# Perceiver-like stack on one core: score tiles of the wide cross-attention issued in pairs, query products over six steps, two waits of TensorE filled

## The chip, the cores and the metric

The kernel runs on one core of a Trainium2 chip, in one launch. The metric is the device time of that launch in microseconds. An execution under the profiler gives the trace; its times are microseconds from the start of the span.

## The reference

Input: latents `x` (8 x 64 x 256) and a context (8 x 1024 x 192). Four blocks, each of a cross-attention, a self-attention and a feed-forward, each with a layer norm before it and a residual add after it:

```python
x = x + _L0_xattn_ref(_layernorm(x), ctx, ...)   # one head
x = x + _L0_attn_ref(_layernorm(x), ...)         # 16 heads of 16, shared keys
x = x + _L0_ffn_ref(_layernorm(x), ...)
x = x + _L1_xattn_ref(_layernorm(x), ctx, ...)   # wide: 16 heads of 64
...
x = x + _L2_xattn_ref(_layernorm(x), ctx, ...)   # wide: 16 heads of 64
```

The change is about the two wide cross-attentions and about `_L0_attn_ref`. A wide one is:

```python
q = (x @ Wq).reshape(b, n, h, d).transpose(0, 2, 1, 3)
k = (context @ Wk).reshape(b, -1, h, d).transpose(0, 2, 1, 3)
v = (context @ Wv).reshape(b, -1, h, d).transpose(0, 2, 1, 3)
attn = softmax(einsum('bhid,bhjd->bhij', q, k) * scale)
out = einsum('bhij,bhjd->bhid', attn, v).transpose(0, 2, 1, 3).reshape(b, n, h * d)
return out @ Wo + bo
```

## The kernel before, in words

The program is written engine by engine, each with its own order of work, written out by hand. Semaphores tie the engines together. `Sync` (SP) issues nearly all DMAs, in one queue.

**The wide layers** (`wide(k)`, k = 0 and 1, on TensorE, ScalarE and VectorE) project the queries through the key weights rather than the context. Eight pairs of heads give queries 0 to 7 (`queries`, L1854). For each head group hh (0 to 7) two products with the key weights (`keys(hh, 0)`, `keys(hh, 1)`, L1874) give the rows that are multiplied with the transposed context. ScalarE makes a high half of them in 16 bits (`keys_high`, L631), VectorE the low half (`keys_low`, L1114). `key_slot` says at which step they are made, `key_banks` in which banks of PSUM.

There are 64 score tiles of 128 rows x 1024 keys, 8 for each head group: tile t = 2g + j, where g is the attention group (32 of them). `scores(t)` (L1890 to L1896) writes banks 2(t%2) and 2(t%2)+1, one bank for each n: in each, four products over 128 rows (h0 and l0 are high and low part of rows 0 to 127 of the context's width, h1 and l1 those of the rest), called whole products here; then one product over 64 rows, with l1, in each bank. These two half products use different halves of the array and run at the same time. Tiles alternate between two pairs of banks, so tile t waits for the exp of tile t-2.

Each tile passes through VectorE and ScalarE: row max (`rowmax`, L1118), `exp` (L639), reciprocal of the sum (`recip`, L1124 and L1125), high part of the weights (`weights_high`, L648), low part (`weights_low`, L1131), then VectorE transposes in blocks (`block_transpose`, L1136). SP stores the tile to DRAM in four pieces (`store_blocks`, L470), and fetches both tiles of a group back, turned (`fetch_turned`, L483). `weights_high(t)` waits for the stores of tile t-3. `attend_high(g)` (L1910 to L1912) and `attend_low(g)` (L1923, in column tiles of 64, and L1929) multiply them with the context; ScalarE copies the result (`attended`, L657). After the four groups of a head group, `heads` (L1942) applies the value weights, VectorE copies that (L1141), and `out` (L1948) applies the output weights at the end.

TensorE's steps s = 0 to 64 in the order of before: `scores(s)`; for s < 3 two queries; `attend_high((s-7)/2)` at odd s from 7, `attend_low((s-8)/2)` at even s from 8; `keys` where `key_slot` is s; `heads(s/8-2)` at multiples of 8 from 16. Then `attend_high(29)`, `attend_low(29)`, `out` of two token tiles, and so on. The output weights (`L1x_o`, `L2x_o`) are loaded by SP after tile 61 has been stored and the fetch of group 30 issued (L458), since they take a slot of the ring that is in use till then. ScalarE and VectorE have steps of the same number: at step s ScalarE does exp and high part of tile s, then a query's scaling (s < 3), `attended`, `keys_high`; VectorE does row max of s, low part of s-1, reciprocal of s, block transpose of s-1, a query's scaling (L1108), `keys_low` at `key_slot`+1, and `heads`.

**Grouped self-attention of block 0** (`self16(0)`) goes through eight units u: `scores(u)` (L2227, L2234), softmax on VectorE and ScalarE, `turn(u)` (a transpose, L2245), `attend(u)`. `project` makes queries, `ready` waits till they are copied. `keep_clock(n, b)` (L1792) issues n matmuls of 512 columns on constants into bank b, whose result nobody reads.

Of the kernel before, what the change touches and what calls it, by code (L numbers as in the profile page):

```python
# [71 lines left out]
def build(nc, widths, units_d, experts_d, const_d, ctx_d, x_d, out_d):  # L72
    ctx = ExitStack()
    with ctx:
# [317 lines left out]
        def key_banks(hh, j):  # L392

            return bank(4 if hh == 0 and j == 1 else 6, 2, 8, 64)

        def key_slot(hh, j):

            return 3 + 2 * j if hh == 1 else 8 * hh - 4 + 2 * j

# [206 lines left out]
        def _(act):  # L606
# [15 lines left out]
            def wide(k):  # L622
# [40 lines left out]
                for s in range(72):  # L663
                    if s < 64:
                        exp(s)
                        weights_high(s)
                    if s < 3:
                        scale_queries(2 * s + 2)
                    if s >= 9 and s % 2 == 1:
                        attended((s - 9) // 2)  # L670
                    for hh in range(1, 8):
                        for j in range(2):
                            if s == key_slot(hh, j):
                                keys_high(hh, j)
# [359 lines left out]
        def _(dve):  # L1034
# [70 lines left out]
            def wide(k):  # L1105
# [41 lines left out]
                for s in range(65):  # L1147
# [6 lines left out]
                    if s >= 1:  # L1154
                        block_transpose(s - 1)
                    if s < 3:
                        scale_queries(2 * s + 3)
                    for hh in range(1, 8):
# [617 lines left out]
        def _(pe):  # L1776
# [63 lines left out]
            def wide(k):  # L1840
# [17 lines left out]
                def keys(hh, j):  # L1858
                    r, hf = 2 * (hh // 2) + j, hh % 2
                    o = key_banks(hh, j)  # L1860
                    if hh == 0:
                        pe.wait_ge(*((xa_qsd, 4 * k + 1) if j else (xa_qsa, 4 * k + 1)))
                        pe.wait_ge(xa_qsd, 4 * k + 1)
                    elif hh == 1:
                        pe.wait_ge(xa_qsa, 4 * k + 4)
                        pe.wait_ge(xa_qsd, 4 * k + 4)
# [11 lines left out]
                def scores(t):  # L1878
# [8 lines left out]
                    h1, l1 = key_columns(k, hh, j, 1, bb)  # L1887
                    for n in range(2):
                        o = ps[:, 2 * (t % 2) + n, :]
                        PE.matmul(o, h0, key_blocks(0, b, n), start=True, stop=False)  # L1890
                        PE.matmul(o, h0, key_blocks(2, b, n), start=False, stop=False)  # L1891
                        PE.matmul(o, l0, key_blocks(0, b, n), start=False, stop=False)  # L1892
                        PE.matmul(o, h1, key_blocks(1, b, n), start=False, stop=False)  # L1893
                    for n in range(2):
                        o = ps[:, 2 * (t % 2) + n, :]
                        ins = PE.matmul(o, l1[half(n)], key_blocks(1, b, n, half(n)), start=False, stop=True)  # L1896
                    ins.then_inc(xa_S, 1)

                def attend_high(g):
                    b = g % 8  # L1900
                    pe.wait_ge(xa_turned[g % 2], turned_value(k, g))
                    if g >= 2:

                        pe.wait_ge(xa_Zs, 32 * k + g - 1)
# [53 lines left out]
                for s in range(65):  # L1958
                    if s < 64:
                        scores(s)  # L1960
                    if s < 3:
                        queries(2 * s + 2)
                        queries(2 * s + 3)
                    if s >= 7 and s % 2 == 1:
# [3 lines left out]
                    for hh in range(1, 8):  # L1968
                        for j in range(2):
                            if s == key_slot(hh, j):  # L1970
                                keys(hh, j)
                                if hh == 7 and j == 1:
                                    pe.wait_ge(xa_A, 16 * k + 16)
                                    release(1)
                    if s >= 16 and s % 8 == 0:
                        if s == 16:
                            loaded(f"{L}_v")
                        heads(s // 8 - 2)
                attend_high(29)
                attend_low(29)  # L1980
                loaded(f"{L}_o")
# [184 lines left out]
            def self16(k):  # L2166
# [105 lines left out]
                if k == 0:  # L2272
# [28 lines left out]
                    shared_values(1, 1)  # L2301
                    project(1, 1, 2, wq, 0)
                    project(1, 1, 2, wq, 1)
                    turn(4)
                    ready(1, 2, 2)
                    scores(6)
# [634 lines left out]
```

## Time and profile before

| what | us |
|---|---|
| median of 3 runs | 1330.73 |
| lowest and highest run | 1323.06, 1332.35 |
| profiled execution, its device time | 1330.26 |
| its span | 1328.5 |
| TensorE matmuls busy | 1244.1 (94% of the span) |
| VectorE busy | 918.6 (69%) |
| ScalarE busy | 616.5 (46%) |
| granted clock of TensorE, mean | 0.982 |

Busy time of TensorE counts a matmul from its start to the end of its pipeline, so matmuls overlap in the rows; how long one takes is read from the start of one to the start of the next. The names are PE for TensorE, PEld for its weight loads, DVE for VectorE, ACT for ScalarE. A row of the timeline may merge several instructions of one line (x8); "[1.43 <-DVE ...]" is idle time ahead of the row and what ended it. An f32 matmul is recorded as two.

### The profile page before, as it was taken

To read this page: it belongs to the slowest core of one execution; us is meant where nothing else is said; L and a number is where in the kernel's file an instruction comes from. 1 tells how busy PE (TensorE), PEld (TensorE's weight loads), DVE (VectorE), ACT (ScalarE), POOL (GpSimd) and SP (SyncE) were. 2 spreads that over 40 slices of the span, in tenths; PEclk is the share of its full clock that TensorE was granted. 3 is DMA by queue.
4 is the path that set the end of the run, shared out by engine and by line. 5 is a ranking of instruction groups with operands and counts; after the bars stand their busy time and mean duration, and the time that the engine had idled before them with its cause. 6 is when DMAs were issued, how large, how long until landed. Compare 5 with 4: busy or idle time off the path is not lost.

```text
span 1328.5 us, 22697 instructions
## 1 busy us (share of the span) xinstructions
PE 1244.1 (94%) x9156; PEld 828.7 (62%) x9156; DVE 918.6 (69%) x1695; ACT 616.5 (46%) x916; POOL 66.9 (5%) x88
## 2 busy tenths in 40 slices
PE   7888899899999999989898899999999999999798
PEld 4556597355555555668584455555555668998375
DVE  7655612799889898345535898989988267882556
ACT  6612311566666666213113666666665024652233
POOL 0000001000000000010001000000000001240100
PEclk9997999999999999999999999999999999999999
DMA  7210164268777767720210577777777514655000
GB/s 259 95 64 1 64 236 176 82 206 252 230 215 222 222 220 225 257 116 1 100 64 32 179 233 232 215 219 223 238 210 242 214 80 177 271 205 203 0 2 17
DMA packets 106072, 215.87 MB, mean 162 GB/s; under 512 B 10864, under 2 KB 76528, under 8 KB 98544
## 3 DMA queue, kind: packets, MB, share of 16 engines
q1 hardware_dynamic: 104816, 206.03, 47.4%
q0 software_dynamic: 1152, 8.39, 1.7%
q8 instruction: 73, 1.20, 0.4%
q14 instruction: 31, 0.25, 0.1%
HBM read 146.74 MB, written 67.63 MB: 161 GB/s over the span
## 4 chain that ended last, share of the span: by engine, by line
PE 70%; DVE 20%; ACT 3%; DMA 2%; issue 2%; POOL 2%; SPq 1%; ACTq 0%; DVEq 0%; POOLq 0%
PE ps L238 20%; PE ps L1910 4%; PE ps L1890 4%; PE ps L1929 4%; PE ps L1911 4%; PE ps L1891 4%; PE ps L1892 4%; PE ps L1893 4%; PE ps L1912 4%; PE ps L1896 3%; PE ps L1854 2%; PE ps L1942 2%; PE ps L1923 2%; PE ps L1874 2%; PE ps L1948 2%
## 5 line engine op out<-in xcount | busy, mean ns | idle before, releaser
L648 ACT ACTIVATE wk<-wk 128x1024 f16<-128x1024 f32 x128 | 185.0, 1445 | 67.4 <-DVE wk L1125 47.0
L639 ACT ACTIVATE wk<-ps,wk 128x1024 f32<-128x1024 f32 x128 | 142.6, 1114 | 149.1 <-DVE wk L1118 149.1
L1118 DVE TENSOR_REDUCE wk<-ps 128x1 f32<-128x1024 f32 x128 | 155.0, 1211 | 54.0 <-PE ps L1896 54.0
L1131 DVE SCALAR_TENSOR_TENSOR wk<-wk 128x1024 f16<-128x1024 f32 x128 | 179.3, 1400 | 4.8 <-ACT wk L648 4.8
L1136 DVE STREAM_TRANSPOSE wk<-wk 128x1024 f32<-128x1024 f32 x128 | 156.9, 1226 | 0.1
L238 PE MATMUL ps<-wk,ring 128*128 128x128 f32 (+4 forms) x920 | 122.1, 290 | 6.7 <-ACT wk L776 2.1
L238 PEld LDWEIGHTS ps<-wk,ring 128*128 128x128 f32 (+1 forms) x920 | 109.3, 192 | 15.9 <-issue 4.8
L238 PE MATMUL ps<-ring,wk 128*128 128x256 f32 (+2 forms) x456 | 100.6, 375 | 3.6 <-DVE wk L1280 1.4
L1890 PE MATMUL ps<-ctx_T,ring 128*128 128x512 f16 x256 | 97.9, 383 | 3.6 <-DVE ring L1114 3.0
L1891 PE MATMUL ps<-ctx_T,ring 128*128 128x512 f16 x256 | 97.6, 381 | 0.0
L1892 PE MATMUL ps<-ctx_T,ring 128*128 128x512 f16 x256 | 97.4, 381 | 0.0
L1893 PE MATMUL ps<-ctx_T,ring 128*128 128x512 f16 x256 | 97.2, 380 | 0.0
L238 PEld LDWEIGHTS ps<-ring,wk 128*128 128x128 f32 (+2 forms) x456 | 79.4, 189 | 15.5 <-DVE wk L1280 1.9
L1792 PE MATMUL ps<-cst 128*128 128x512 f16 x318 | 79.5, 396 | 9.7 <-DMA cst<-consts 6.9
L1910 PE MATMUL ps<-ring,ctx_keys 128*128 128x256 f16 x320 | 87.6, 274 | 0.0
L1911 PE MATMUL ps<-ring,ctx_keys 128*128 128x256 f16 x320 | 87.2, 273 | 0.0
L1912 PE MATMUL ps<-ring,ctx_keys 128*128 128x256 f16 x320 | 86.2, 269 | 0.0
L541 POOL TENSOR_TENSOR rstd<-rstd,cst 128x3 f32<-128x3 f32 (+1 forms) x26 | 19.5, 753 | 1158.2 <-DVE rstd L1051 1151.8
L238 PE MATMUL ps<-xn_both,ring 128*128 128x256 f32 (+2 forms) x220 | 59.0, 425 | 3.9 <-DVE xn_both L1083 3.9
L657 ACT ACTIVATE wk<-ps 128x512 f32<-128x512 f32 x64 | 36.5, 570 | 54.6 <-PE ps L1929 48.7
L1792 PEld LDWEIGHTS ps<-cst 128*128 128x128 f16 x318 | 30.6, 101 | 47.5 <-issue 11.3
L238 PE MATMUL ps<-wk 128*32 128x64 f32 (+7 forms) x676 | 56.6, 250 | 3.8 <-ACT wk L799 2.0
(344 smaller groups left out, 2080.2 us busy)
## 6 DMA issues: line engine op xcount, KB each, us to landing
blocks<-wk SPq DMA_DIRECT2D x512, 128.0 KB, 3.9
ring<-blocks SPq DMA_DIRECT2D x40, 1024.0 KB, 5.7
ring<-units SPq DMA_DIRECT2D x34, 1024.0 KB, 6.1
xn_both<-blocks SPq DMA_DIRECT2D x22, 1024.0 KB, 5.7
ring<-experts SPq DMA_DIRECT2D x16, 1024.0 KB, 5.3
ring<-context SPq DMA_DIRECT2D x16, 384.0 KB, 4.0
wk<-context SPq DMA_DIRECT2D x16, 384.0 KB, 5.2
wk<-blocks SPq DMA_DIRECT2D x2, 1024.0 KB, 5.0
```

Of the source, the lines that this page charges most:

```text
L238: return PE.matmul(out, lhsT, rhs, start=start, stop=stop)
L639: ACTE.activation(blocks, bank(2 * (t % 2), 2, 4, 128), ACT.Exp, bias=WNM[:, t % 4:t % 4 + 1], accum_out=WRS[:, t % 4:t % 4 + 1]).then_inc ...
L648: ACTE.activation(weight_halves(t)[0], WXP[:, t % 2, :], ACT.Identity, scale=WRI[:, t % 4:t % 4 + 1]).then_inc(xa_PH, 1)
L1118: DVE.tensor_reduce(WNM[:, t % 4:t % 4 + 1], bank(2 * (t % 2), 1024), X, ALU.max, negate=True).then_inc(xa_max, 1)
L1131: DVE.scalar_tensor_tensor(low, WXP[:, t % 2, :], WRI[:, t % 4:t % 4 + 1], high, ALU.mult, ALU.subtract).then_inc(xa_PL, 1)
L1136: DVE.transpose(packed_weights(t), packed_weights(t)).then_inc(xa_block, 1)
L1890: PE.matmul(o, h0, key_blocks(0, b, n), start=True, stop=False)
L1891: PE.matmul(o, h0, key_blocks(2, b, n), start=False, stop=False)
L1892: PE.matmul(o, l0, key_blocks(0, b, n), start=False, stop=False)
L1893: PE.matmul(o, h1, key_blocks(1, b, n), start=False, stop=False)
L1910: PE.matmul(z1, CN[:, kt, hi:hi + 128], h, start=n == 0, stop=False)
L1911: PE.matmul(z1, CN[:, kt, lo:lo + 128], h, start=False, stop=False)
```

## The change

Six things are changed.

1. TensorE issues `scores(s)` and `scores(s+1)` back to back at even s. The even tile has its half products last, the odd tile first, so that the four half products of a pair are adjacent.
2. Queries 2 to 7 come one at each of steps 0 to 5, not two at each of steps 0 to 2; their scaling on ScalarE (even ones) and VectorE (odd ones) moves with them.
3. `keys(1, 0)` uses bank 4, so it no longer waits for the queries' scaling; `keys(1, 1)` moves from step 5 to step 6. `attend_high(0)`, which writes bank 4, waits for `keys_low(1, 0)`.
4. `heads(6)` comes after `attend_high(29)`.
5. In `self16(0)` there are six `keep_clock` matmuls ahead of the second half of a projection, and
6. four after `turn(4)`, with a wait for `sa_ys`, because they write the bank that `attend` uses.

```diff
--- before.py
+++ after.py
@@ -391,11 +391,11 @@
 
         def key_banks(hh, j):
 
-            return bank(4 if hh == 0 and j == 1 else 6, 2, 8, 64)
+            return bank(4 if (hh, j) in ((0, 1), (1, 0)) else 6, 2, 8, 64)
 
         def key_slot(hh, j):
 
-            return 3 + 2 * j if hh == 1 else 8 * hh - 4 + 2 * j
+            return 3 + 3 * j if hh == 1 else 8 * hh - 4 + 2 * j
 
         def hi_columns(g):
 
@@ -664,8 +664,8 @@
                     if s < 64:
                         exp(s)
                         weights_high(s)
-                    if s < 3:
-                        scale_queries(2 * s + 2)
+                    if s < 6 and s % 2 == 0:
+                        scale_queries(s + 2)
                     if s >= 9 and s % 2 == 1:
                         attended((s - 9) // 2)
                     for hh in range(1, 8):
@@ -1153,8 +1153,8 @@
                         recip(s)
                     if s >= 1:
                         block_transpose(s - 1)
-                    if s < 3:
-                        scale_queries(2 * s + 3)
+                    if s < 6 and s % 2 == 1:
+                        scale_queries(s + 2)
                     for hh in range(1, 8):
                         for j in range(2):
                             if s == key_slot(hh, j) + 1:
@@ -1861,7 +1861,7 @@
                     if hh == 0:
                         pe.wait_ge(*((xa_qsd, 4 * k + 1) if j else (xa_qsa, 4 * k + 1)))
                         pe.wait_ge(xa_qsd, 4 * k + 1)
-                    elif hh == 1:
+                    elif hh == 1 and j == 1:
                         pe.wait_ge(xa_qsa, 4 * k + 4)
                         pe.wait_ge(xa_qsd, 4 * k + 4)
                     if hh >= 2:
@@ -1885,20 +1885,34 @@
                         pe.wait_ge(xa_exp, 64 * k + t - 1)
                     h0, l0 = key_columns(k, hh, j, 0, bb)
                     h1, l1 = key_columns(k, hh, j, 1, bb)
-                    for n in range(2):
-                        o = ps[:, 2 * (t % 2) + n, :]
-                        PE.matmul(o, h0, key_blocks(0, b, n), start=True, stop=False)
-                        PE.matmul(o, h0, key_blocks(2, b, n), start=False, stop=False)
-                        PE.matmul(o, l0, key_blocks(0, b, n), start=False, stop=False)
-                        PE.matmul(o, h1, key_blocks(1, b, n), start=False, stop=False)
-                    for n in range(2):
-                        o = ps[:, 2 * (t % 2) + n, :]
-                        ins = PE.matmul(o, l1[half(n)], key_blocks(1, b, n, half(n)), start=False, stop=True)
-                    ins.then_inc(xa_S, 1)
+                    odd = t % 2 == 1
+
+                    def whole():
+                        for n in range(2):
+                            o = ps[:, 2 * (t % 2) + n, :]
+                            PE.matmul(o, h0, key_blocks(0, b, n), start=not odd, stop=False)
+                            PE.matmul(o, h0, key_blocks(2, b, n), start=False, stop=False)
+                            PE.matmul(o, l0, key_blocks(0, b, n), start=False, stop=False)
+                            ins = PE.matmul(o, h1, key_blocks(1, b, n), start=False, stop=odd)
+                        return ins
+
+                    def halves():
+                        for n in range(2):
+                            o = ps[:, 2 * (t % 2) + n, :]
+                            ins = PE.matmul(o, l1[half(n)], key_blocks(1, b, n, half(n)), start=odd, stop=not odd)
+                        return ins
+                    if odd:
+                        halves()
+                        whole().then_inc(xa_S, 1)
+                    else:
+                        whole()
+                        halves().then_inc(xa_S, 1)
 
                 def attend_high(g):
                     b = g % 8
                     pe.wait_ge(xa_turned[g % 2], turned_value(k, g))
+                    if g == 0:
+                        pe.wait_ge(xa_AL, 16 * k + 3)
                     if g >= 2:
 
                         pe.wait_ge(xa_Zs, 32 * k + g - 1)
@@ -1956,11 +1970,11 @@
                 keys(0, 0)
                 keys(0, 1)
                 for s in range(65):
-                    if s < 64:
+                    if s < 64 and s % 2 == 0:
                         scores(s)
-                    if s < 3:
-                        queries(2 * s + 2)
-                        queries(2 * s + 3)
+                        scores(s + 1)
+                    if s < 6:
+                        queries(s + 2)
                     if s >= 7 and s % 2 == 1:
                         attend_high((s - 7) // 2)
                     if s >= 8 and s % 2 == 0:
@@ -1972,11 +1986,12 @@
                                 if hh == 7 and j == 1:
                                     pe.wait_ge(xa_A, 16 * k + 16)
                                     release(1)
-                    if s >= 16 and s % 8 == 0:
+                    if s >= 16 and s % 8 == 0 and s < 64:
                         if s == 16:
                             loaded(f"{L}_v")
                         heads(s // 8 - 2)
                 attend_high(29)
+                heads(6)
                 attend_low(29)
                 loaded(f"{L}_o")
                 pe.wait_ge(xa_Hs, 8 * k + 7)
@@ -2300,8 +2315,11 @@
                     attend(3)
                     shared_values(1, 1)
                     project(1, 1, 2, wq, 0)
+                    keep_clock(6, 5)
                     project(1, 1, 2, wq, 1)
                     turn(4)
+                    pe.wait_ge(sa_ys, 2 * k + 1)
+                    keep_clock(4, 4)
                     ready(1, 2, 2)
                     scores(6)
                     attend(4)
```

## Rows read from the trace of the kernel before

**Rows 1.** Windows: stretch, busy us (instructions) of each engine, clock, DMA share, GB/s; middle.

```profile
306.00:540.00 234.00, 233.33 (x1674) 136.88 (x1674) 211.07 (x267) 152.67 (x187) 0.00 (x0) 1.00 0.74 225
```

**Rows 2.** Timeline of PE at the first wide layer's start: start, us, idle before.

```profile
239.44 3.70 PE L1854 MATMUL ps<-xn_both,ring 128*128 128x512 f32 x8
...
265.71 1.47 PE L1874 MATMUL ps<-wk,ring 64*128 64x256 f32 x8 [3.99 <-DVE ring L1114]
...
280.82 0.39 PE L1896 MATMUL ps<-ctx_T,ring 64*128 64x512 f16 x2
...
305.93 1.13 PE L1874 MATMUL ps<-wk,ring 64*128 64x256 f32 x8 [0.33 <-DVE ring L1114]
```

**Rows 3.** Timeline of DVE over the same stretch.

```profile
242.23 0.17 DVE L1125 RECIPROCAL wk<-wk 128x1 f32<-128x1 f32 x1
...
245.23 1.23 DVE L1118 TENSOR_REDUCE wk<-ps 128x1 f32<-128x1024 f32 x1 [1.36 <-PE ps L1896]
...
249.14 0.65 DVE L1108 TENSOR_SCALAR wk<-ps 128x512 f32<-128x512 f32 x1
...
279.60 1.19 DVE L1118 TENSOR_REDUCE wk<-ps 128x1 f32<-128x1024 f32 x1
...
283.47 1.18 DVE L1118 TENSOR_REDUCE wk<-ps 128x1 f32<-128x1024 f32 x1
...
304.59 1.19 DVE L1114 TENSOR_TENSOR ring<-ps,ring 128x1024 f16<-128x1024 f32 x1
```

**Rows 4.** Timeline of PE at the ends of both wide layers.

```profile
540.75 1.95 PE L1942 MATMUL ps<-wk,ring 128*64 128x256 f32 x16 [1.10 <-ACT wk L657]
...
548.64 7.17 PE L1948 MATMUL ps<-ring,wk 128*128 128x256 f32 x32 [1.61 <-DMA ring<-units]
...
1023.74 3.35 PE L1942 MATMUL ps<-wk,ring 128*64 128x256 f32 x16 [2.02 <-ACT wk L657]
...
1031.49 7.16 PE L1948 MATMUL ps<-ring,wk 128*128 128x256 f32 x32
```

**Rows 5.** Timeline of SP's queue at the second layer's end.

```profile
1023.63 0.41 SPq L458 DMA_DIRECT2D ring<-units  x1
```

**Rows 6.** DMA issues in the window of that issue: KB, us to landing.

```profile
ring<-units SPq DMA_DIRECT2D x1, 1024.0 KB, 7.8
```

**Rows 7.** Timeline of PE in the first layer's middle, tiles one after the other.

```profile
509.66 0.39 PE L1896 MATMUL ps<-ctx_T,ring 64*128 64x512 f16 x2
509.99 0.29 PE L1910 MATMUL ps<-xn_both,ctx_keys 128*128 128x256 f16 x1
...
512.66 0.38 PE L1890 MATMUL ps<-ctx_T,ring 128*128 128x512 f16 x1
...
513.96 0.38 PE L1892 MATMUL ps<-ctx_T,ring 128*128 128x512 f16 x1
514.17 0.38 PE L1893 MATMUL ps<-ctx_T,ring 128*128 128x512 f16 x1
514.48 0.39 PE L1896 MATMUL ps<-ctx_T,ring 64*128 64x512 f16 x2
514.80 0.63 PE L1923 MATMUL ps<-xn_both,ctx_keys 128*64 128x256 f16 x8
...
516.27 0.38 PE L1890 MATMUL ps<-ctx_T,ring 128*128 128x512 f16 x1
```

**Rows 8.** Costliest groups: count, busy and mean ns, idle before and its releaser.

```profile
L639 ACT ACTIVATE wk<-ps,wk 128x1024 f32<-128x1024 f32 x128 | 142.6, 1114 | 149.1 <-DVE wk L1118 149.1
```

**Rows 9.** Timeline of PE in grouped self-attention of block 0.

```profile
114.98 1.13 PE L238 MATMUL ps<-wk,ring 128*128 128x256 f32 x4 [1.43 <-DVE wk L1337]
...
117.43 0.38 PE L2227 MATMUL ps<-wk 128*128 128x256 bf16 x2 [0.89 <-issue]
```

**Rows 10.** Windows: busy time and granted clock of a stretch of the same layer.

```profile
119.70:129.80 10.10, 9.79 (x72) 7.64 (x67) 7.15 (x14) 2.00 (x4) 0.00 (x0) 0.50 0.00 1
```

**Rows 11.** Groups by line of ACT between 275 and 530 us.

```profile
L648 ACT ACTIVATE wk<-wk 128x1024 f16<-128x1024 f32 x55 | 79.5, 1446 | 28.1 <-DVE wk L1125 20.6 <-DMA blocks<-wk 7.5
```

## Prediction

> **What bounds the kernel now.** I read the windows first, then the timeline of TensorE for what it waited for, then those of VectorE and SP beside it. In the long middle of a wide layer TensorE is busy 233.3 of 234 us at full clock, and VectorE 211 [rows 1]: there TensorE is the bound, and its pieces count one by one. VectorE has the rest of the time as slack, 23 us or a tenth, and a faster TensorE is passed on until that is used.
>
> The start of a wide layer differs. There `keys(1,1)` waits 3.99 us for VectorE's `keys_low` [rows 2], and from then on VectorE goes from tile to tile every 3.87 us without a gap (279.60, 283.47) [rows 3] and lags TensorE until `keys(2,1)`, which waits a last 0.33 us [rows 2]. So up to score tile 14 the layer is set by VectorE, and it idled ahead of that: its row max at 245.23 had waited 1.36 us for TensorE's half products [rows 3].
>
> At the end `heads(6)` waits 1.10 us in the first wide layer and 2.02 us in the second, and `out(0)` waits 1.61 us for the output weights in the first and nothing in the second [rows 4]. But in the second, the load of those weights is issued at 1023.63 and takes 7.8 us, to 1031.43 [rows 5, 6], and `out(0)` starts at 1031.49: it came just in time. In both layers the weights are what `out(0)` can't pass.
>
> **Part 1, halves adjacent and tiles paired.** Whole products follow each other by 0.21 us (513.96, 514.17). From the last whole product to the halves it is 0.31, so the switch costs 0.10; halves to the column-tiled matmuls of `attend_low` 0.32 where the two concurrent halves take 0.22, again 0.10; halves to `attend_high` 509.66 to 509.99, 0.33, so 0.11 [rows 7]. A pair of tiles has four such changes before and three after: (in, out, in, out) becomes (in, out) and one from whole products to `attend_low`. Saving 0.10 us a pair, if a change from whole products to column tiles costs what the others do, and if the second pair of halves follows the first at 0.22. Bounds for the latter: 0 extra, as two halves start together, and 0.10 extra, the whole of the gain, if each pair waits for its weights as after a switch. I take 0: the 64-row matmuls of `keys` are 8 in 1.13 us [rows 2], so they run on without such gaps. From tile 14 to tile 60, 24 pairs: 2.4 us a layer, 4.8 us.
>
> **Part 2, what pairing does to waits.** Score tile s+1 is now issued before `attend_low` (1.47 us, 514.80 to 516.27) [rows 7] and needs `exp(s-1)`; `attend_high` takes 2.67 us (509.99 to 512.66) [rows 7]. From the halves of tile s-2 to the start of tile s+1 TensorE has 4.2 + 1.5 + 2.7 + 2.1 minus the first halves, about 8.4 us. `exp(s-1)` is done 0.4 + 3.9 (VectorE's tile) + 1.1 (row max) + 1.3 (exp, 1.11 and its sum read out) [rows 8] = 6.7 us after them. Slack 1.7: no wait. One wait is tight. Tile 8h+1 needs `keys_low(h,1)`, and `keys(h,1)` comes after tiles 8h-2 and 8h-1, so TensorE has 0.22 + 0.32 + 1.8 + 1.5 + 1.1 + 2.7 + 1.8 + 0.2 = 9.6 us from the halves of 8h-2. VectorE needs 0.4 + 2 x 3.87 + 1.2 (`keys_low`) [rows 3] = 9.3, and 0.1 to 0.4 more where ScalarE's cast of the keys stands before the next exp. Bounds 0 and 0.5 us for each; behind the waiting scores stand `attend_low` and `heads`, and VectorE waits for nothing but the scores. I take 0.2 for each of 6 head groups a layer: 2.4 us lost in all. Before, `attend_low` and `heads` stood ahead of that tile and covered it.
>
> **Part 3, the start.** I walk the new order from the first scores at 237.3. Tiles 0 and 1 to 241.4; queries 2 and 3 (3.70 for two by their row, 3.54 from start to start) [rows 2] to 245.0; tiles 2, 3 to 249.1; queries 4, 5 and `keys(1,0)`, in its new bank so that it waits for no query, to 253.7; tiles 4, 5, then 6 after queries 6, 7 to 263.4. VectorE: the first reciprocal is at 242.23 [rows 3], and now tile 1's row max follows at once, where it came at 245.23. Then 3.9 a tile, 0.65 more where it scales a query, 1.1 where it does `keys_low` [rows 3]: row max 2 at 247.3, 3 at 251.2, 4 at 255.9, 5 at 260.9, 6 at 265.4, 7 at 269.3; `keys_low(1,1)` ends 274.3, and row max 8 starts there instead of at 279.60 [rows 3]. TensorE: tile 7 and `keys(1,1)` to 266.6, `attend_high(0)` to 269.3, tile 8 to 271.3. Then tile 9 waits for `keys_low(1,1)` until 274.4: a stall of 3.1 us in place of the 3.99 [rows 2]. Tile 9, `attend_low(0)`, `attend_high(1)` bring tile 10 to 280.7. Before, tile 9's halves were at 280.82 [rows 2], and tile 10 began 0.3 + 2.7 later, at 283.8. Gain 3.1, and the 0.33 of `keys(2,1)` goes too, because VectorE is 4 to 5 us earlier: 3.4 a layer. The clock takes some back. After the 3.99 us the eight matmuls of `keys(1,1)` took 1.47 against 1.13 at full clock [rows 2], and that loss is in the time of before. I expect a stall of 3.1 us to bring the clock down too, and to give back 1.5, as much as the slow stretch after `heads(6)` cost (3.35 against 1.95, and 0.1 on what followed) [rows 4]. Net 1.9 a layer, 3.8 us; bounds 0 (VectorE doesn't get ahead) and 3.4 (no drop).
>
> **Part 4, `attend_high(29)` ahead of `heads(6)`.** It fills the wait of 1.10 and 2.02 us. But `out(0)` can't start before its weights have landed, and their load is released by VectorE's tile 61 and its stores, which pairing doesn't move, since VectorE's 3.87 a tile, not TensorE, sets tile 61. So what is filled comes back ahead of `out(0)`: a pause of about 1.6 + 1.2 = 2.8 us in the first layer and 3.8 in the second. Gain nothing. In the trace the pauses of 3.99 and 2.02 us were followed by matmuls at half clock (1.2 GHz, by the durations), those of 1.10 and 1.61 were not [rows 2, 4]. So I expect `out(0)` (7.17 us for 32 matmuls) to begin at 1.2 GHz and lose what `heads(6)` lost, 1.5 us: 3.0 us lost in two layers; bounds 0 and 3.4.
>
> **Part 5, the fillers in grouped self-attention.** Ten matmuls at 0.22 us, 2.2 us, lie in waits of 1.43 and 0.89 us [rows 9]; if that cover were gone they would cost these 2.2. The added wait (`sa_ys`) is one that `attend(4)` makes anyway, and ScalarE's copy is long done; behind it stand `ready`, `scores(6)`. What they may bring: from 119.7 to 129.8 TensorE is busy 9.79 us at a granted clock of 0.50 [rows 10], so at most 4.9. I take half, 2.5, since that stretch ends in turns that await ScalarE and VectorE; bounds -2.2 and 4.9.
>
> **Sum.** 4.8 - 2.4 + 3.8 - 3.0 + 2.5 = 5.7 us. The profiled execution took 1330.26 (span 1328.5), 0.5 below the median of three, 1330.73. Forecast 1324.5.
>
> **Rivals.**
> A. The clock holds: neither tile 9's stall nor the pause ahead of `out(0)` brings it down, and the fillers work whole. 4.8 - 2.4 + 6.8 + 0 + 4.9 = 14.1: 1316. For it: 1.61 us brought no drop. Against: 3.99 and 2.02 did [rows 2, 4].
> B. The second pair of halves waits for its weights, 0.10 us for each pair of tiles: the 4.8 goes, 1329.3. For it: no row of before has two pairs of halves in a row. Against: `keys` [rows 2]. The Trainium skill (TensorE: Matmul & The Clock Gate, Part 3, "The mechanism") says that weight loads overlap matmuls in flight only where the row group differs; the second pair has the row groups of the first, so by that rule this rival would hold, at 1329.3. The 64-row `keys` of this trace, which reuse their row groups without a gap, speak against it.
> C. The fillers do nothing for the clock: 2.5 goes, 1327.
> D. Slower: the tight wait of part 2 decides. ScalarE waits for stored blocks now and then, 7.5 us in 55 tiles [rows 11]. If such a wait falls in the step of `keys_low(h,1)` it is added to tile 8h+1's stall, which nothing covers now. At 1.0 us for each of 12 head groups it costs 12: 1336.5. It decides from 0.5 us each on. Against: the mean is 7.5/55 = 0.14 a tile.
>
> **How the numbers follow.** Forecast 0.47 (own range 1320 to 1329), A 0.14, B 0.15, C 0.17, D 0.07. The range holds A and B and goes 2 to 3 us past them, since the three runs of before lie 9 us apart (1323.06 to 1332.35) without any change, and leaves out most of D: 1313 to 1333. A measurement of this kernel tells about 1% from no change, 13.3 us. Faster by more needs 1317.4 or less, which is most of A and a sliver of the forecast: 0.14. Slower by over 1% (1344) is the far end of D: 0.03. The rest, 0.83, is within 1%.
>
> **What would show it.** Steps: pairs of tiles 8.32 us apart instead of 8.42, four halves in two starts 0.22 apart; a wait of tile 9 on `keys_low` of about 3 us where `keys(1,1)` had 3.99; row max 8 some 5 us earlier; waits of 0 to 0.5 us at tiles 17, 25 and so on; `heads(6)` without a wait and `out(0)` with 3 to 4 us on its weights; full clock from 119.7 on. It is wrong if the halves stand 0.3 apart, if tile 9 doesn't wait, or if `out(0)` starts earlier against tile 60 than before.

## The result, and the profile after

The changed kernel takes 1313.99 us (median of 4 runs, 1308.78 to 1319.69); the kernel before took 1326.89 beside it (4 runs, 1322.81 to 1332.35). The ratio is 0.988, with a 95% interval of 0.985 to 0.992. Measured a second time, with more runs, it is 0.990 (0.988 to 0.993; 1316.44 against 1330.91). By the medians the change is worth 12.9 and 14.5 us, by the ratios 16 and 13; the forecast was 5.7. The kernel before has no single time: over four sets its median lies between 1326.9 and 1330.9.

The profiled execution took 1317.12, 13.1 less than the profiled one of before. The head of its page, TensorE's row and its clock in 40 slices:

```profile
span 1315.3 us, 22717 instructions
...
PE 1235.5 (94%) x9166; PEld 822.5 (63%) x9166; DVE 918.2 (70%) x1695; ACT 619.0 (47%) x916; POOL 66.9 (5%) x88
...
PEclk9999999999999999999999999999999999999999
```

TensorE is as busy as before in share, and it is 8.6 us less in sum. No slice's mean falls below 9 tenths now, where before slice 4 had 7. The clock still fell in nine short stretches, as the sum below says. Where the time went is seen from the starts of the same instructions in both traces. The stages of a wide layer are: from tile 0 to row max 16 ("start"), eight tiles of the middle (row max 32 to 40), row max 16 to 60, row max 60 to `out(0)`, and `out(0)` to TensorE's first transpose of the next layer norm ("tail"). Each number is a difference of two starts, in us, for the first and the second wide layer:

```
kernel         start        8 tiles       16 to 60       60 to out(0)  tail
before         77.30 76.69  38.01 38.01   208.75 209.29  25.30 26.07   28.79 28.78
changed        74.36 74.39  37.80 37.80   207.95 207.95  24.88 25.71   28.79 28.69
changed_again  74.47 72.81  37.79 37.79   207.92 207.90  24.95 26.52   28.79 28.79
fill_only      77.71 76.48  38.01 38.01   209.06 209.30  26.30 26.59   28.79 28.68
no_fillers     72.81 72.81  37.80 37.80   208.12 207.97  25.03 26.16   28.79 28.79
heads_back     74.40 72.82  37.80 37.80   207.96 207.96  25.12 25.45   28.79 28.79
halves_apart   75.31 73.81  38.19 38.17   210.15 210.06  25.05 26.51   28.79 28.79
start_only     74.99 73.35  38.01 38.01   209.06 209.06  26.82 26.58   28.79 28.68
pair_only      75.47 76.81  37.79 37.79   207.91 207.91  25.24 25.73   28.78 28.79
low_first      71.68 71.69  37.57 37.57   206.88 206.81  25.00 26.60   28.79 28.78
fill9          72.81 73.48  37.80 37.79   207.96 208.05  26.39 26.13   28.79 30.47
copy_first     74.45 75.67  37.79 37.79   207.92 207.93  25.48 26.73   31.67 31.67
low_first_al0  70.85 70.84  37.57 37.57   206.81 206.81  25.34 25.80   28.79 28.79
all_three      71.58 71.47  37.57 37.57   206.08 206.18  25.50 26.51   28.79 30.47
```

The middle, in PE's timeline (start, us, instruction; the rows that answer to [rows 7]):

```profile
366.22 0.38 PE L1895 MATMUL ps<-ctx_T,ring 128*128 128x512 f16 x1
366.44 0.38 PE L1896 MATMUL ps<-ctx_T,ring 128*128 128x512 f16 x1
366.75 0.63 PE L1937 MATMUL ps<-xn_both,ctx_keys 128*64 128x256 f16 x8
...
373.55 0.38 PE L1896 MATMUL ps<-ctx_T,ring 128*128 128x512 f16 x1
373.86 0.61 PE L1902 MATMUL ps<-ctx_T,ring 64*128 64x512 f16 x4
374.40 0.39 PE L1893 MATMUL ps<-ctx_T,ring 128*128 128x512 f16 x1
```

The four halves start at 373.86 and the odd tile's whole products 0.54 later: the second pair starts at 374.09, so 0.23 for one pair and 0.31 for the other and the way out. The second pair does not wait for its weights: all four loads are done within 0.11 us, while the first pair runs.

```profile
373.86 0.11 PEld L1902 LDWEIGHTS ps<-ctx_T,ring 64*128 64x128 f16 x4 [0.42 <-issue]
```

From whole products to the column tiles it is 0.31 (366.44 to 366.75), 0.10 over the plain distance, as the other switches.

The start, PE first and then DVE ([rows 2, 3]):

```profile
267.65 0.39 PE L1902 MATMUL ps<-ctx_T,ring 64*128 64x512 f16 x2
270.83 0.60 PE L1902 MATMUL ps<-ctx_T,ring 64*128 64x512 f16 x2 [2.79 <-DVE ring L1114]
...
274.53 0.63 PE L1937 MATMUL ps<-wk,ctx_keys 128*64 128x256 f16 x8
```

```profile
238.77 0.17 DVE L1125 RECIPROCAL wk<-wk 128x1 f32<-128x1 f32 x1
238.85 1.21 DVE L1118 TENSOR_REDUCE wk<-ps 128x1 f32<-128x1024 f32 x1
...
243.39 0.65 DVE L1108 TENSOR_SCALAR wk<-ps 128x512 f32<-128x512 f32 x1
243.96 1.21 DVE L1118 TENSOR_REDUCE wk<-ps 128x1 f32<-128x1024 f32 x1
...
270.70 1.21 DVE L1118 TENSOR_REDUCE wk<-ps 128x1 f32<-128x1024 f32 x1
```

Tile 9's halves wait 2.79 us for `keys_low`, where `keys(1,1)` waited 3.99. The second row max follows the first reciprocal at once (238.77, 238.85), and row max 8 is 36.9 us after tile 0, not 42.3. Column tiles of `attend_low(0)` come 3.70 us after those halves, where full clock takes 2.15 (in fill9 below, 274.21 to 276.36): the clock is down there.

The ends ([rows 4]), and the issue of the second layer's output weights ([rows 5]), which took 7.7 us to land:

```profile
533.39 0.27 PE L1924 MATMUL ps<-ring,ctx_keys 128*128 128x256 f16 x1 [1.16 <-ACT wk L657]
...
536.14 1.95 PE L1956 MATMUL ps<-wk,ring 128*64 128x256 f32 x16
...
541.02 4.15 PE L1962 MATMUL ps<-ring,wk 128*128 128x256 f32 x18 [1.49 <-DMA ring<-units]
...
1010.56 0.27 PE L1924 MATMUL ps<-ring,ctx_keys 128*128 128x256 f16 x1 [1.98 <-ACT wk L657]
...
1014.95 1.95 PE L1956 MATMUL ps<-wk,ring 128*64 128x256 f32 x16
...
1018.18 1.03 PE L1962 MATMUL ps<-ring,wk 128*128 128x256 f32 x4
```

```profile
1010.36 0.41 SPq L458 DMA_DIRECT2D ring<-units  x1
```

Here the trace departs from the forecast: `attend_high(29)` waits 1.16 and 1.98 us, for the same copy by ScalarE (L657) that `heads(6)` waited for. `out(0)` waits 1.49 us in the first layer and nothing in the second, much as before (1.61 and nothing), and it runs at full clock.

### The profile page after: what moved, and what is told of

The parts are those of the page before. It is cut to its first block, busy times and chain, and to the rows that moved or that the text cites. A ratio compares the mean times of both kernels' runs of the same rounds, so it can differ in the third digit from the quotient of the medians.

```text
span 1315.3 us, 22717 instructions
## 1 busy us (share of the span) xinstructions
PE 1235.5 (94%) x9166; PEld 822.5 (63%) x9166; DVE 918.2 (70%) x1695; ACT 619.0 (47%) x916; POOL 66.9 (5%) x88
## 4 chain that ended last, share of the span: by engine, by line
PE 68%; DVE 21%; ACT 4%; issue 2%; DMA 2%; POOL 2%; SPq 0%; ACTq 0%; DVEq 0%; POOLq 0%
PE ps L238 19%; PE ps L1943 4%; PE ps L1924 4%; PE ps L1893 4%; PE ps L1925 4%; PE ps L1926 4%; PE ps L1894 3%; PE ps L1895 3%; PE ps L1896 3%; PE ps L1937 3%; PE ps L1902 2%; PE ps L1956 2%; PE ps L1874 2%; PE ps L1962 2%; PE ps L1792 2%
## 5 line engine op out<-in xcount | busy, mean ns | idle before, releaser
L1792 PE MATMUL ps<-cst 128*128 128x512 f16 x328 | 83.8, 402 | 10.0 <-DMA cst<-consts 6.6
L657 ACT ACTIVATE wk<-ps 128x512 f32<-128x512 f32 x64 | 36.6, 571 | 54.3 <-PE ps L1943 42.5
L238 PE MATMUL ps<-xn_both,ring 128*128 128x256 f32 (+2 forms) x220 | 54.7, 403 | 4.1 <-DVE xn_both L1083 3.9
```

Source lines behind the costliest of these rows:

```text
L238: return PE.matmul(out, lhsT, rhs, start=start, stop=stop)
L1792: PE.matmul(ps[:, b, :], cst[:, 0:64].bitcast(F16), cst[:, 0:256].bitcast(F16), start=True, stop=True)
```

## The experiments

All ratios are to the kernel before, measured on the same chip in the same set of runs; those of one set of four share its runs.

**fill_only**: before, with the fillers added.

```diff
+                    keep_clock(6, 5)
                     project(1, 1, 2, wq, 1)
                     turn(4)
+                    pe.wait_ge(sa_ys, 2 * k + 1)
+                    keep_clock(4, 4)
```

> The kernel before plus the ten fillers in grouped self-attention, nothing else. Theory 1 (the fillers keep the clock up and the half-clock stretch from 119.7 to 129.8 us goes): the layer's last turn comes 4.4 us earlier than before, as in the changed kernel (there turn(6) was 4.4 us earlier), and the time is about 4 us below before, ratio 0.997. Theory 2 (that gain was the phase of the clock in one execution and not the fillers): turn(6) within 0.5 us of before and ratio 1.000.

Measured: 1.0015 (0.9988 to 1.0041), 1330.60 us against 1327.71.

**no_fillers**: changed, with these lines taken out.

> The changed kernel without the ten fillers; the wide layers as changed. Theory 1: the half-clock stretch is back in the second half of the grouped layer, turn(6) is within 0.5 us of before, and the time is some 4 us above the changed kernel: ratio to before 0.991 to 0.992. Theory 2 (phase only): the layer is as fast as in the changed kernel, ratio 0.988. In both the wide layers keep their gain of 4 us each.

Measured: 0.991 (0.988 to 0.994), 1313.25 us. The changed kernel had 0.988 and 0.990, in two other sets. The ratio of fill_only shuts out the 0.997 of its theory 1; that of no_fillers holds theory 1's 0.991 to 0.992 and, just, theory 2's 0.988, so it decides nothing. The single profiles went theory 1's way: `turn(6)` begins 55.9 us after the second layer norm before and 51.9 in fill_only, 49.7 in the changed kernel and 56.1 in no_fillers, where the half-clock stretch of 10.2 us from 119.7 on is back. More profiles take the edge off this. The windows from 102 to 136 us (PE, PEld, DVE, ACT, POOL busy, granted clock, DMA share, GB/s) of, in this order, fill_only, no_fillers, the changed kernel and low_first_al0, of which all but no_fillers have the fillers:

```profile
102.00:136.00 34.00, 28.86 (x319) 21.30 (x319) 20.88 (x42) 8.84 (x16) 0.86 (x1) 0.90 0.00 1
```

```profile
102.00:136.00 34.00, 28.73 (x304) 22.67 (x304) 18.36 (x33) 8.40 (x16) 0.00 (x0) 0.80 0.00 1
```

```profile
102.00:136.00 34.00, 30.05 (x336) 22.05 (x336) 21.74 (x46) 8.73 (x16) 1.52 (x2) 0.95 0.12 42
```

```profile
102.00:136.00 34.00, 31.52 (x309) 24.29 (x308) 18.32 (x33) 8.07 (x14) 0.00 (x0) 0.70 0.00 1
```

With the fillers in, much the same code sees a clock of 0.95, 0.90 or 0.70 there. From TensorE's first transpose of the second layer norm to its first of the third, this part takes 58.5, 61.8 to 62.0 or 65.3 us with the fillers (ten profiles: 2, 6 and 2 of them, mean 61.9) and 61.9 to 64.7 without (four profiles, mean 63.8). How the slow stretches fall is different from one execution to the next. A gain of some 2 us on average would fit these profiles. The times don't show it: the interval of fill_only leaves room for 1.6 us.

**heads_back**: changed, but

```diff
-                    if s >= 16 and s % 8 == 0 and s < 64:
+                    if s >= 16 and s % 8 == 0:
...
                 attend_high(29)
-                heads(6)
                 attend_low(29)
```

> The changed kernel with heads(6) again ahead of attend_high(29). Theory 1 (both wait for the same copy by ScalarE, attended(27), so the order fills nothing, and out(0) waits for its weights anyway): the pause of 1.2 us in the first layer and 2.0 in the second stands ahead of heads(6) instead, out(0) starts at the same distance from row max 60 within 0.2 us, ratio as the changed kernel, 0.988. Theory 2 (the order filled a wait and gave 1 to 2 us a layer): out(0) comes 1 to 2 us later in each layer, ratio 0.990 to 0.991.

Measured: 0.992 (0.989 to 0.995), 1314.84 us; `out(0)` 25.12 and 25.45 us after row max 60, against 24.88 and 25.71. PE, ahead of `heads(6)` in both layers and `out(0)` in the second:

```profile
532.32 1.95 PE L1956 MATMUL ps<-wk,ring 128*64 128x256 f32 x16 [1.33 <-ACT wk L657]
...
1003.33 1.95 PE L1956 MATMUL ps<-wk,ring 128*64 128x256 f32 x16 [1.81 <-ACT wk L657]
...
1010.87 7.17 PE L1962 MATMUL ps<-ring,wk 128*128 128x256 f32 x32 [1.26 <-DMA ring<-units]
```

The wait is the same one, it only stands elsewhere. Theory 1 holds by the trace: the order fills nothing, and `out(0)` is within 0.3 us of the changed kernel, where theory 2 had it 1 to 2 us later. The ratio alone could not tell, as its interval holds theory 2's 0.990 to 0.991.

**halves_apart**: changed, but odd tiles as even ones.

```diff
-                    if odd:
-                        halves()
-                        whole().then_inc(xa_S, 1)
-                    else:
-                        whole()
-                        halves().then_inc(xa_S, 1)
+                    whole()
+                    halves().then_inc(xa_S, 1)
```

> The changed kernel, scores still in pairs, but the odd tile too has its half products last, so the halves of a pair are no longer adjacent. Theory 1 (the gain in the middle is the changes of array tiling saved): pairs without keys or heads take 8.42 us instead of 8.31, eight tiles 38.1 instead of 37.8, the time is 3 to 5 us above the changed kernel, ratio 0.991 to 0.992. Theory 2 (the pairing, not the adjacency, is what helps): pairs stay at 8.31 and the ratio at 0.988.

Measured: 0.997 (0.995 to 0.999), 1323.23 us. PE:

```profile
347.04 0.38 PE L1896 MATMUL ps<-ctx_T,ring 128*128 128x512 f16 x1
347.35 0.39 PE L1902 MATMUL ps<-ctx_T,ring 64*128 64x512 f16 x2
347.78 0.39 PE L1893 MATMUL ps<-ctx_T,ring 128*128 128x512 f16 x1
...
349.31 0.38 PE L1896 MATMUL ps<-ctx_T,ring 128*128 128x512 f16 x1
349.62 0.39 PE L1902 MATMUL ps<-ctx_T,ring 64*128 64x512 f16 x2
349.94 0.65 PE L1933 MATMUL ps<-ring,ctx_keys 128*64 128x256 f16 x8
```

The halves come in twos, the way out into a whole product is even 0.43 here. Pairs take 8.44 us and eight tiles 38.19: theory 1. The adjacency is worth 2.2 us a layer in the middle and 1 at the start, 6.3 us in all; pairs without it are slower in the middle than no pairs at all (210.1 us from row max 16 to 60, against 209.1). By the time it is more than the 3 to 5 us that I gave it: 1323.23 against 1313.25 us of no_fillers in the same set. Of these 10 us the wide layers show 6.3; where the rest comes from is open.

**changed_again**: no edit.

> The changed kernel once more, unedited, to have it on the same chip and with as many executions as its variants. Theory 1 (the execution profiled before the change was 2.5 us above the median of 23, and the fillers are worth nothing on average): ratio 0.989 to 0.991, about 1314 us, level with the version without fillers. Theory 2 (the fillers are worth their 4 us): ratio 0.987 or less and clearly below the version without them.

Measured: 0.990 (0.988 to 0.993), 1316.44 us. Level with no_fillers (0.991); theory 1, as far as ratios that are each uncertain by 3 to 4 us can say.

**start_only**: before, with the query steps, `key_banks` and `key_slot` of the change and the waits that go with them.

> The kernel before with the new start alone: queries over six steps, keys(1,0) in bank 4, keys(1,1) at step 6; scores one by one, halves at their end, no fillers. Theory 1 (the gain of the start is VectorE's second row max coming earlier, and a query between tiles 0 and 1 in place of two already gives most of it): row max 1 is 1.8 us earlier against tile 0, row max 8 some 4 us earlier, the stage from tile 0 to row max 16 takes 3 us less than the 77.3 and 76.7 of before; the middle stays at 38.0 us for eight tiles; ratio 0.995. Theory 2 (the pairing gives the gain of the start): the stage is within 1 us of before, ratio 0.999.

Measured: 0.996 (0.994 to 0.998), 1324.20 us. DVE, first reciprocal and second row max:

```profile
243.38 0.16 DVE L1125 RECIPROCAL wk<-wk 128x1 f32<-128x1 f32 x1
244.66 1.23 DVE L1118 TENSOR_REDUCE wk<-ps 128x1 f32<-128x1024 f32 x1 [1.12 <-PE ps L1896]
```

**pair_only**: before, with `scores(s)`, `scores(s + 1)` at even s and the halves adjacent.

> The kernel before with the scores in pairs and the four halves adjacent, but the queries still two at each of the first three steps, keys(1,0) and keys(1,1) where they were, no fillers. Theory 1: eight tiles of the middle take 37.8 us against 38.0, 1.3 us a layer; at the start row max 1 comes 2.8 us earlier too, but keys(1,0) and (1,1) share banks and wait, so the stage to row max 16 gains 1 to 3 us; ratio 0.995 to 0.997. Theory 2 (nearly all of the change is the pairing): ratio 0.991 or less and the start as fast as in the changed kernel (74.4).

Measured: 0.996 (0.993 to 0.998), 1324.29 us. DVE:

```profile
241.95 0.16 DVE L1125 RECIPROCAL wk<-wk 128x1 f32<-128x1 f32 x1
244.75 0.69 DVE L1108 TENSOR_SCALAR wk<-ps 128x512 f32<-128x512 f32 x1 [2.63 <-PE ps L1854]
245.35 1.21 DVE L1118 TENSOR_REDUCE wk<-ps 128x1 f32<-128x1024 f32 x1
```

Each alone is worth 5 to 6 us by the ratios, 11 together, near the 13 of the whole change in this set. At the start they are not equal. One query between tiles lets the row max of tile 1 come at 244.66, 6.23 us after tile 0 in place of 7.95, with 1.12 us of waiting, and that gives nearly the whole gain: tile 0 to row max 16 takes 74.99 us where the clock falls and 73.35 where it holds, against 74.4 and 72.8 in the changed kernel and 77.05 on average before. So theory 1 of start_only holds. Pairs without it are no better than before (76.81 us where the clock falls): the scaling of query 3 (L1108) stands ahead of row max 1 in VectorE's step and waits 2.63 us for a product that now comes after both tiles. I had put row max 1 at 2.8 us earlier there; it is 0.4 us later than before against tile 0 (8.35 to 7.95 us). Together they give 5.03.

pair_only also shows the same pause with and without a fall of the clock, ahead of `keys(1,1)` in its two layers: 1.95 us for the eight matmuls against 1.13. That is why its first layer took 75.47.

```profile
265.43 1.13 PE L1874 MATMUL ps<-wk,ring 64*128 64x256 f32 x8 [3.59 <-DVE ring L1114]
...
741.46 1.95 PE L1874 MATMUL ps<-wk,ring 64*128 64x256 f32 x8 [3.59 <-DVE ring L1114]
```

**low_first**: changed, with `keys_low` ahead of `block_transpose` in VectorE's step.

> The changed kernel with keys_low ahead of the block transpose in VectorE's step, so that it ends 1.15 us sooner. Theory 1 (tile 8h+1 waits 0.2 us for keys_low in each head group, tile 9 waits 2.8): the wait of tile 9 shrinks to 1.7 us, those of tiles 17, 25 and so on vanish, eight tiles take 37.55 us against 37.80; with the pause below 2 us the clock holds more often; 3 to 5 us below the changed kernel, ratio 0.986 to 0.987. Theory 2 (the stores of the transposed tile come later and ScalarE's wait for them takes the place): eight tiles stay at 37.8 or rise, ratio 0.990.

Measured: 0.988 (0.986 to 0.990), 1313.93 us against 1316.44 of the changed kernel in the same set. DVE, then the wait of tile 9 on PE:

```profile
270.86 0.16 DVE L1125 RECIPROCAL wk<-wk 128x1 f32<-128x1 f32 x1
270.94 1.21 DVE L1114 TENSOR_TENSOR ring<-ps,ring 128x1024 f16<-128x1024 f32 x1
272.06 1.24 DVE L1136 STREAM_TRANSPOSE wk<-wk 128x1024 f32<-128x1024 f32 x1
```

```profile
272.20 0.39 PE L1902 MATMUL ps<-ctx_T,ring 64*128 64x512 f16 x2 [1.65 <-DVE ring L1114]
```

Theory 1 for the waits: 1.65 us at tile 9 where I had 1.7, eight tiles in 37.57 us where I had 37.55. That is what the tight wait cost: 0.23 us in each head group. The time fell by 2.5 us and not by 3 to 5, a difference that the intervals can't tell from either, nor from none.

**fill9**: changed, with `keep_clock(12, 5)` between tiles 8 and 9.

> The changed kernel with twelve filler matmuls (2.6 us at 0.22 each) between tiles 8 and 9, in the wait of 2.79 us for keys_low. Theory 1 (the clock falls after that pause in some executions and costs 1.6 us each time; in the profiles of the changed score order so far it did in 4 of 8 layers): with the pause filled the stage from tile 0 to row max 16 is 72.8 to 73.1 us in both layers of the profile, never 74.4, and the time is 1 to 2 us below the changed kernel, ratio 0.989. Theory 2 (the clock falls anyway, or the fillers delay tile 9): 74.4 or more in a layer, ratio 0.991.

Measured: 0.992 (0.989 to 0.995), 1318.83 us. PE:

```profile
271.03 0.39 PE L1902 MATMUL ps<-ctx_T,ring 64*128 64x512 f16 x2
271.35 2.76 PE L1792 MATMUL ps<-cst 128*128 128x512 f16 x12
274.21 0.39 PE L1902 MATMUL ps<-ctx_T,ring 64*128 64x512 f16 x2
...
276.36 0.63 PE L1937 MATMUL ps<-wk,ctx_keys 128*64 128x256 f16 x8
```

The pause is filled without a wait, the stage is 72.81 and 73.48, and the clock did not fall there in either layer, but no gain shows in the time: inconclusive. Two layers without a fall prove little, since it stayed away in 5 of 12 without the fillers too. In the second layer tile 17 waited 0.84 us, hence the 73.48. What a clock drop costs here is known from the table, 72.8 against 74.4 of the same code.

**copy_first**: changed, with

```diff
                         exp(s)
+                        if s == 63:
+                            attended(27)
                         weights_high(s)
...
-                    if s >= 9 and s % 2 == 1:
+                    if s >= 9 and s % 2 == 1 and s != 63:
                         attended((s - 9) // 2)
```

> The changed kernel with ScalarE's copy attended(27) ahead of weights_high(63), so that neither attend_high(29) nor heads(6), which both wait for that copy, has to wait 1.2 and 2.0 us. Theory 1 (out(0) is bound by the landing of its weights, 7.7 us after an issue that follows the stores of tile 61): attend_high(29) starts without a wait, out(0) waits that much longer, and out(0) stays 24.9 to 26.5 us after row max 60; ratio as the changed kernel, 0.990. Theory 2 (the wait that was filled decides): out(0) 1.2 and 2.0 us earlier, ratio 0.988.

Measured: 0.994 (0.992 to 0.996), 1324.02 us, so 0.4 to 0.6% (5 to 8 us) worse than the changed kernel by the ratios. PE, `out(0)` of both layers:

```profile
548.55 10.06 PE L1964 MATMUL ps<-ring,wk 128*128 128x256 f32 x32 [3.41 <-DMA ring<-units]
...
1026.41 10.06 PE L1964 MATMUL ps<-ring,wk 128*128 128x256 f32 x32 [4.66 <-DMA ring<-units]
```

Now the wait is really filled, and what the forecast said of it comes true: a pause of 3.41 and 4.66 us ahead of `out(0)`, which starts no earlier (25.48 and 26.73), and then runs slowly, 10.06 us against the 7.17 of [rows 4]. The tail grows from 28.79 to 31.67, 2.9 us in each layer. The profiled execution, 1328.10 us, was the slowest of the twelve, so the usual loss may be smaller.

**low_first_al0**: low_first, with

```diff
                         scores(s)
+                        if s == 8:
+                            attend_low(0)
                         scores(s + 1)
...
-                    if s >= 8 and s % 2 == 0:
+                    if s > 8 and s % 2 == 0:
```

> keys_low ahead of the block transpose, and attend_low(0) between tiles 8 and 9, in the 1.65 us that tile 9 still waits there. Theory 1 (up to tile 10 TensorE, after tile 9 it is the bound again): the wait of tile 9 falls to 0.2 us, the stage to row max 16 takes 70.2 to 70.5 us against 71.7 with keys_low first alone, 1.3 us a layer; ratio 0.986. Theory 2 (VectorE, which goes from tile to tile without a gap there, is the bound up to tile 16): the stage stays at 71.7, ratio 0.988.

Measured: 0.984 (0.981 to 0.987), 1312.57 us against 1329.77. PE:

```profile
272.85 0.39 PE L1902 MATMUL ps<-ctx_T,ring 64*128 64x512 f16 x2
273.17 0.64 PE L1937 MATMUL ps<-wk,ctx_keys 128*64 128x256 f16 x8
273.74 1.06 PE L1943 MATMUL ps<-wk,ctx_keys 128*128 128x256 f16 x8
274.90 0.39 PE L1902 MATMUL ps<-ctx_T,ring 64*128 64x512 f16 x2
```

The best version of the study: 0.4 to 0.6% below the changed kernel by the ratios. The stage takes 70.85 us, 0.8 less than low_first, between the two theories. In all_three, whose start is the same code, it takes 71.5, near theory 2's 71.7; but from tile 0 to row max 60 both versions take 277.7 us, and low_first 278.5. So the gain is 0.9 us a layer, and row max 16 is a poor mark for it.

**all_three**: low_first_al0 with copy_first's edit.

> keys_low first, attend_low(0) between tiles 8 and 9, and attended(27) ahead of weights_high(63) together. Theory 1: the sum of the parts, ratio 0.985 to 0.986, out(0) still 25 to 26.5 us after row max 60. Theory 2 (out(0) is no longer bound by its weights once the copy is early): out(0) at 23.5 to 24.5 us after row max 60, ratio 0.984 or less.

Measured: 0.989 (0.986 to 0.992), 1315.71 us: worse than without the early copy. `out(0)` is no earlier (25.50, 26.51), after pauses of 3.42 and 4.44 us. The tail of the second layer grew to 30.47; that of the first stayed at 28.79, at full clock behind the 3.42 us, where copy_first lost 2.9 behind 3.41. So the early copy costs half a per cent by the ratios again (3 us by the medians), of which the tails show 1.7 us; the rest is not accounted for.

## Why the prediction fell short

The direction was right and the size was not: 5.7 us forecast, 13 to 16 measured. By its parts:

- **Part 1 and 2, the middle: right.** 4.8 - 2.4 = 2.4 us forecast (tile 14 to 60 are 23 pairs, not 24, so 4.6). Row max 16 to 60 went from a mean of 209.10 (before and fill_only, four layers) to 207.97 (changed, changed_again, no_fillers, six layers): 1.1 a layer, 2.2 us. A switch of tiling costs 0.10 us, the pair gains 0.11, the tight wait costs 0.2; halves_apart and low_first show each by itself. Rival B was wrong: the four halves went in 0.23 + 0.31 us, their weights hidden. Rival D did not come about. The rule cited for B, of the Trainium skill (TensorE: Matmul & The Clock Gate, Part 3, "The mechanism"), that weight loads overlap matmuls in flight only where the row group differs, doesn't describe this pair: the second pair's weights went into row groups whose matmuls were running (373.86 to 373.97).
- **Part 3, the start: the mechanism right, the size too small.** The walk gave row max 8 37.0 us after tile 0; it is 36.9. It gave a wait of 3.1 us; it is 2.79. Forecast 3.8 us for both layers, measured about 7: from a mean of 77.05 (four layers) to 73.61 (eight: the three above and heads_back). The term that was mis-sized is the clock, the 1.5 us given back in each layer. The walk put tile 10 at 43.4 us after tile 0 with the clock held and, with those 1.5, at 44.9; measured are 43.3 and 44.9, against 46.4 to 47.7 before. I took the clock to fall each time. In the profiles whose tile 9 has this wait (2.79 us, 2.88 in halves_apart) it fell in 7 of 12 layers and not in the others (in the changed code 74.4 us and 72.8), while before it fell in all four after the 3.99 us. Of the eight layers of the mean it fell in four, so the term should have been 0.8 on average. The rest of the miss lies behind tile 10, where I gave only the 0.33 of `keys(2,1)`: from there to row max 16 it is 0.8 us less, 29.5 in place of 30.1 to 30.8. Three pairs of 0.11 us, which Part 1 counts from tile 14 on only, are part of that.
- **Part 4, the step that failed.** "It fills the wait of 1.10 and 2.02 us" is false. `attend_high(g)` waits for `xa_Zs` at 32k+g-1, which for g = 29 is 28, and `heads(6)` waits for 4 x 6 + 4 = 28: the same copy. Nothing was filled, so the pause ahead of `out(0)` did not grow (1.49 us and none, where I had 2.8 and 3.8), and the 3.0 us that I charged for a slow `out(0)` were not lost. This error and that of Part 3, 3 us each, make up most of the miss. My own sign of being wrong came up too: `out(0)` started 0.4 us earlier against row max 60 in both layers of the changed kernel's profile, on average over the profiles 0.5 (26.07 to 25.54). It is spread more than effect. `out(0)` starts 7.8 to 8.0 us after its weights are issued (L458) in all these layers, and the issue, which waits for tile 61's stores to land, comes 17.0 to 18.8 us after row max 60 in the changed score order and 17.5 to 18.7 before; the 0.11 us of the pair is the only part of it that the new order explains. The reasoning behind the charge was right in kind: with the wait really filled, 2.9 us were lost in both layers of copy_first, and 0 and 1.7 in all_three.
- **Part 5, the fillers: not shown to help.** 2.5 us forecast; the times of fill_only leave room for 1.6 at most, the profiles say 2. Rival C is the nearer case.
- **The sum.** Middle 2.2, start 6.9, fillers 0 to 2, and 1.0 at the end that may be chance: 9 to 12 us, at the lower end of the two intervals (9 to 16 us from the second, 11 to 20 from the first). What is left is not shown by any run. Where the clock falls in the rest of the kernel is enough to hide or make it: outside the wide layers the same code differs by up to 5 us from profile to profile (between the two wide layers 125.2 to 130.1 us), and the profile that the forecast stood on had 12 slow stretches, the changed kernel's 9.

The range held the median, 1313.99, at its very edge, and that was luck: it had been made wide for the spread of the runs. Rival A came nearest, with 1316, but the clock held at tile 9 in half of the layers only, and the fillers did not work whole.

## What to carry to other kernels

If two instructions seem to offer each other cover, compare the values that they wait for, not only their names: a reorder fills a wait only when what is moved up waits for something earlier. A pause in TensorE costs more than its length when it brings the clock down; between 1.8 and 3.6 us that was a matter of chance here, so a forecast should give it a chance and not a yes or no. And filling one pause may only merge it with the next one; whether the wait that comes after is bound by a transfer decides. Last, try the parts of a change alone before giving each its share: at the start the spread queries gave nearly everything and the pairs nothing until the queries were spread, because VectorE's second row max stood behind a scaling that waited for them.

## What the runs showed of the hardware

- A pause of 2.79 or 2.88 us was followed by half clock in 7 of 12 layers, with the same code where it was and where it wasn't. One of 3.59 us was followed by it in one of two layers (pair_only), and so was one of 1.79 us (start_only: the eight matmuls behind it took 1.94 us in one layer and 1.14 in the other). The 3.41 us of copy_first were, the 3.42 of all_three were not. Those of 3.99 us (four layers), 4.44 and 4.66 were each time, those of 1.65 in neither layer of low_first. So the length of the pause alone does not decide it.
- The same part of the program takes 58.5, 61.9 or 65.3 us by where the slow stretches fall, and a profiled execution lay up to 5.1 us from the median of its runs (heads_back, 1309.71 against 1314.84): more than most of the terms that one would read from it.
- Two pairs of 64-row matmuls on the same halves of the array follow each other at 0.23 us, with their weights loaded meanwhile; going from one tiling to another costs 0.10 us each time, 0.21 in one case (from halves back to whole products within a pair, 347.35 to 347.78).
